# Two attention layers around a state-space block: the scan with tokens on partitions, its segment decays made beside the convolution, the decay rates spread by VectorE

## What is computed

```python
def _mamba2_block(x, norm_w, in_proj_w, conv_w, conv_b, dt_bias, A_log, D_skip, gnorm_w, out_proj_w):
    zxbcdt = _rms(x, norm_w) @ in_proj_w
    z = zxbcdt[..., :D_INNER]                       # 512 wide
    xBC = zxbcdt[..., D_INNER:D_INNER + CONV_DIM]   # 768 wide: x, B, C
    dt = jax.nn.softplus(zxbcdt[..., -H_M:] + dt_bias)        # 8 heads
    conv = conv_b + sum((padded[:, k:k + L, :] * conv_w[:, k] for k in range(D_CONV)))   # 4 taps
    xBC = jax.nn.silu(conv)
    decay = jnp.exp(dt * A)
    dbx = dt[..., None] * xh
    def step(h, inp):
        dec, u, bt, ct = inp
        h = h * dec[:, :, None, None] + u[..., None] * bt[:, None, None, :]
        return (h, jnp.einsum('bhpn,bn->bhp', h, ct))
    y = ys.transpose(1, 0, 2, 3) + D_skip[None, None, :, None] * xh
    u = _rms(y.reshape(b, L, D_INNER) * jax.nn.silu(z), gnorm_w)
    return resid + u @ out_proj_w
```

## Time and profile before

| | us |
|---|---|
| median of 3 runs | 9226.33 |
| lowest, highest | 9217.38, 9246.14 |
| the profiled execution, its own time | 9249.62 |
| the span of the profile | 9247.8 |
| busy: PE, DVE, ACT, POOL | 7938.6, 5014.7, 3326.8, 1960.8 |

### The profile page before, as it was taken

How to read it: one execution, slowest core, us unless ns; L and a number is a source line. 1 busy time by engine, 2 the same in 40 slices (tenths; PEclk the granted TensorE clock), 3 DMA queues, 4 the chain that set the end, 5 groups by cost and what they waited for, 6 DMA issues and landing times.

```text
span 9247.8 us, 129067 instructions
## 1 busy us (share of the span) xinstructions
PE 7938.6 (86%) x37700; PEld 3524.7 (38%) x38020; DVE 5014.7 (54%) x12781; ACT 3326.8 (36%) x4038; POOL 1960.8 (21%) x1802
## 2 busy tenths in 40 slices
PE   3979799897998979889798897979989798897988
PEld 0343433434333343333434334343343433334343
DVE  3555364654645556454564656536465464555546
ACT  0424334242342424424243342433424234242442
POOL 3040130302203031130311304013030221303113
PEclk5989889898998989989799898989989899898998
DMA  3142231323313132041422303223131330313213
GB/s 73 20 74 35 41 60 20 65 33 48 53 19 70 28 57 51 12 75 23 69 39 26 71 17 69 35 43 57 20 69 30 50 58 12 70 28 64 45 19 72
DMA packets 216597, 421.47 MB, mean 46 GB/s; under 512 B 35542, under 2 KB 126584, under 8 KB 215812
## 3 DMA queue, kind: packets, MB, share of 16 engines
q1 hardware_dynamic: 213841, 412.14, 25.9%
q10 hardware_dynamic: 2048, 0.53, 0.0%
HBM read 190.14 MB, written 8.51 MB: 21 GB/s over the span
## 4 chain that ended last, share of the span: by engine, by line
PE 59%; issue 14%; DVE 13%; DMA 6%; POOL 4%; ACT 2%; SPq 2%; DVEq 0%; ACTq 0%; POOLq 0%
PE ps L1004 13%; PE ps L941 10%; PE ps L975 8%; PE ps L977 6%; PE ps L903 5%; DVE mx L1588 5%; PE ps L979 4%; PE ps L1009 4%; DMA stage<-in_mask 3%; PE ps L1124 2%; DMA qst<-q1hl 2%; PE ps L960 2%; PE ps L1040 2%; DVE xc L1716 1%; ACT PR L1362 1%
## 5 line engine op out<-in xcount | busy, mean ns | idle before, releaser
L1362 ACT ACTIVATE PR<-ps 128x1024 f32<-128x1024 f32 x2496 | 2504.0, 1025 | 2634.8 <-PE ps L977 1514.2
L1559 DVE CUSTOM_DVE_ANT_0 ps<-ps,maskq 128x402 f32<-128x402 f32 x4203 | 2408.3, 587 | 1567.1 <-PE ps L941 1375.8
L1004 PE MATMUL ps<-PR,vbuf 128*32 128x512 f32 x9984 | 1356.6, 616 | 5.2 <-ACT PR L1362 5.2
L977 PE MATMUL ps<-maskk,identb 128*128 128x512 bf16 x3008 | 1147.6, 382 | 0.0
L941 PE MATMUL ps<-kst,qst 96*128 96x402 bf16 (+1 forms) x3115 | 1026.0, 342 | 115.6 <-DVE mx L1559 89.9
L1588 DVE TENSOR_REDUCE mx<-ps 128x2 f32<-128x804 f32 x1024 | 933.3, 988 | 314.1 <-PE ps L960 312.7
L960 PE MATMUL ps<-kst,qst 100*128 100x402 f32 x2048 | 753.3, 495 | 360.8 <-DMA qst<-q1hl 254.4
L975 PE MATMUL ps<-qst,kst 99*128 99x512 bf16 x2496 | 956.7, 383 | 7.3
L979 PE MATMUL ps<-qst,kst 102*128 102x512 f32 x1664 | 768.0, 526 | 100.3 <-ACT PR L1362 71.0
L941 PEld LDWEIGHTS ps<-kst,qst 96*128 96x128 bf16 x3115 | 282.4, 97 | 1209.7 <-DVE mx L1559 819.4
L722 POOL MEMSET qst<- 3x2048 f32 (+1 forms) x34 | 47.5, 1398 | 3117.7 <-PE ps L1004 3071.1
(11 more groups left out here) (194 smaller groups left out, 8046.4 us busy)
## 6 DMA issues: line engine op xcount, KB each, us to landing
kst<-khl SPq DMA_DIRECT2D x96, 800.5 KB, 17.0
kst<-khl SPq DMA_DIRECT2D x300, 200.1 KB, 7.6
stage<-in_maskt SPq DMA_DIRECT2D x204, 256.0 KB
stage<-in_mask SPq DMA_DIRECT2D x204, 201.0 KB
ctxs<-in_ctxt SPq DMA_DIRECT2D x17, 1601.0 KB, 9.7
qst<-q1hl SPq DMA_DIRECT2D x96, 256.0 KB, 12.1
win_s<-in_w_in SPq DMA_DIRECT2D x16, 1288.0 KB, 5.9
KS<-khl SPq DMA_DIRECT2D x102, 200.1 KB
```

What stands on the lines that cost most here:

```text
L977: mm = pe.matmul(o, identb[:, :], maskk[:, t, :], start=False, stop=True)
L1004: mm = pe.matmul(ps[32 * j:32 * j + 32, 6, :], l, PR[:, t % 2, j, :], start=(t == 0), stop=(t == KT - 1), tile_position=(0, 32 * j))
L1362: nc.scalar.activation(PR[:, t % 2, 2 * half:2 * half + 2, :], ps[:, 2 * half:2 * half + 2, :], ACT.Exp, scale=scale).then_inc(s_p, 1)
L1559: nc.vector.tensor_tensor_reduce(src, src, maskq[:, i, c0:c0 + w], 1.0, -3.0e38, ALU.add, ALU.max, mx[:, c, h * QT + i:h * QT + i + 1]).th ...
```

## The change

The scan's y now comes out with tokens on partitions, in the layout of the residual rows. The weight on the state is no longer a 128 x 1024 tensor per chunk but a factor per token and head (a third block of `dec`), applied after the matmul of C with `Hst`; the second sums, the second exponentials and the GpSimd product are gone. The skip term is a matmul with a diagonal matrix (`dskd`). z is projected with tokens on partitions. The gated rows are squared and summed on ScalarE, transposed by TensorE, copied by ScalarE and projected (`project_block(c)`) inside the loop.

All four triangles of decays are made beside the convolution: `aU` is filled by VectorE (`spread_a`, after the convolution steps in `A_STEPS`), and the exponentials go to `windows`, which lies on the memory of `qst`. The last tap and the bias of the convolution are made by ScalarE from PSUM, so VectorE runs three taps. All of `SECOND` is projected before the scan (`FILL0`, `FILL_AT`): 8 tiles before the transposes, then one after each projection j, three after the last.

Around it: the sums of the first attention are spread over partitions by four matmuls over 128 rows without waits between them, after the first tile of `project_out`; LayerNorm takes two operations a tile in place of three; the roots are taken in parts; the k parts on GpSimd come after the first roots; SyncE loads 2 mask pieces early and not 4, and waits for the sums (`s_D`), not for the end of the scan (`s_g`), before the next x; constant rows of the q stack, which `windows` overwrites, are written again from DRAM (`rows_q1`); the second q projection starts on three of the four row tiles.

```diff
--- before.py
+++ after.py
-        OUT_BANK = [0, 1, 3, 2]
+        OUT_BANK = [5, 7, 6, 3]
+        A_STEPS = [0, 3, 5, 6]
+        FILL0 = V_LN + 1
+        FILL_AT = [1] * (NCH + XT) + [3]
...
-        PIECE1, FRONT_PIECES, ROW1_STEP = 4, 2, 4
+        PIECE1, PIECE2, FRONT_PIECES, ROW1_STEP = 2, 4, 2, 4
...
-                sp.wait_ge(s_g, QT * (b + 1))
+                load_pieces(b, bn, 0, PIECE1, False)
+                sp.wait_ge(s_D, QT * (b + 1))
                 alone(sp)
                 load_xt(bn)
-                load_pieces(b, bn, 0, PIECE1, False)
                 sp.wait_ge(s_vfree, (b + 1) * KT)
                 alone(sp)
                 load_ctx(bn)
+                rows_q1(b)
                 for g in range(G1):
                     stack_q1(b, g)
...
-                if i == 0:
-                    pe.wait_ge(s_rs, b * NG + gi + 1)
-                else:
-                    pe.wait_ge(s_spread, n + i)
-                r = slice(32 * i, 32 * i + 32)
-                pe.matmul(ps[:, 7, i * P:(i + 1) * P], sel[r, :], rsm[r, :], start=True, stop=True,
-                          tile_position=(32 * i, 0)).then_inc(s_spread, 1)
+                pe.wait_ge(s_rs, b * NG + gi + 1)
+                for i in range(QT):
+                    mm = pe.matmul(ps[:, 7, i * P:(i + 1) * P], sel[:, i, :], rsm[:, :], start=True, stop=True)
+                mm.then_inc(s_spread, 1)
...
                     mm.then_inc(s_in, 1)
-                fill(V_IN)
+                    fill(FILL_AT[j])
+                    if NCH - 2 <= j < NCH + 2:
+                        window_sums(b, j - NCH + 2)
...
                 for c in range(QT):
                     cs = slice(c * P, (c + 1) * P)
                     nb = b * QT + c
                     if c > 0:
-                        window_sums(b, c)
+                        pe.wait_ge(s_h, LEAD + b * (QT - 1) + c)
...
+                        pe.matmul(ps[:, 3, :], xc[:, NCH - 1, cs], Hst[:, :], start=True, stop=True).then_inc(s_zi, 1)
...
                     for i in range(XT):
+                        pe.matmul(ps[:, 2, i * P:(i + 1) * P], xc[:, i, cs], dskd[:, i, :], start=(i == 0), stop=False)
                     pe.wait_ge(s_M, nb + 1)
                     pe.wait_ge(s_dx, nb + 1)
                     for h in range(HM):
+                        mm = pe.matmul(ps[:, 2, h * PD:(h + 1) * PD], window(c)[:, h, :], dx[:, h * PD:(h + 1) * PD],
+                                       start=False, stop=(h == HM - 1))
                     mm.then_inc(s_yp, 1)
                     if c < QT - 1:
+                        x_tokens(c + 1)
                         pe.wait_ge(s_dx2, b * (QT - 1) + c + 1)
...
+                        pe.matmul(ps[:, 4, :], btok[:, c, :], dx2[:, :], start=True, stop=True).then_inc(s_hp, 1)
+                    if c > 0:
+                        project_block(c - 1)
...
+                    nc.scalar.activation(xc[:, ch, :], ps[:, bank, :], ACT.Identity, bias=cb_c[:, ch:ch + 1],
+                                         scale=cw_c[:, ch * TAPS + TAPS - 1:(ch + 1) * TAPS])
                     nc.scalar.activation(rawc[:, n % 2, TAPS - 1:TAPS - 1 + T], ps[:, bank, :], ACT.Copy)\
                         .then_inc(s_rawcp, 1)
...
+                for n in range(NCH):
+                    gate(n)
+                    if n + 2 < NCH:
+                        copy_raw(n + 2)
+                    fill(FILL_AT[n + 3])
+                    if n == 0:
+                        act.wait_ge(s_dps, b + 1)
+                        nc.scalar.activation(dec[:, :, :].rearrange("p a n -> p (a n)"),
+                                             ps[:, 4, 0:3 * QT * HM], ACT.Exp).then_inc(s_dec, 1)
+                    elif n <= QT:
+                        window_decays(b, n - 1)
...
+                def spread_a(c):
+                    if c > 0:
+                        dve.wait_ge(s_D, b * QT + c)
+                    else:
+                        dve.wait_ge(s_a, b + 1)
+                    nc.vector.tensor_tensor(
+                        aU[:, :, :], aa[:, c, :].unsqueeze(2).broadcast_to([P, HM, P]),
+                        upto[:, :].unsqueeze(1).broadcast_to([P, HM, P]), ALU.mult).then_inc(s_au, 1)
+
                 for n in range(NCH + 1):
                     if n < NCH:
                         convolve(n)
+                    if n in A_STEPS:
+                        spread_a(A_STEPS.index(n))
                     if n >= 1:
                         gate_conv(n - 1)
```

More of the change, by code:

```diff
@@ L294, in xattn_mamba @@
         s_rstd = sem("s_rstd")
[L295 removed]
+        s_ln = [sem(f"s_ln{i}") for i in range(2)]
         s_sq = sem("s_sq")
@@ L1110, in _, with project_q1 @@
                 second = list(SECOND)
+                def project_q1(item, lo, hi):
+                    i = item[2]
+                    for k in range(DT):
+                        mm = pe.matmul(ps[:, pj_bank[item], lo:hi], wq1_s[:, k, i * P:(i + 1) * P], xn[:, k, lo:hi],
+                                       start=(k == 0), stop=(k == DT - 1))
+                    return mm
                 def fill(n):
@@ new lines, in _ @@
+                    if NCH - 2 <= j < NCH + 2:
+                        window_sums(b, j - NCH + 2)
+                assert not second
+                pe.wait_ge(s_xc, b * NCH + 2)
+                pe.wait_ge(s_vfree, (b + 1) * KT)
+                pe.wait_ge(s_rest, rests(b, K1[-1]) + 1)
+                for c in range(QT):
+                    cs = slice(c * P, (c + 1) * P)
+                    mm = pe.matmul(ps[:, 6, cs], xc[:, NCH - 2, cs], xc[:, NCH - 1, cs], start=True, stop=True)
+                mm.then_inc(s_G, 1)
```

536 lines of the change are left out of this document (275 added, 261 removed).

## The result

The changed kernel takes **8713.95 us** (median of 4 runs, 8706.96 to 8720.84) where the kernel before takes 9225.26 (4 runs beside it, 9217.38 to 9246.14): ratio **0.9442, 95% interval 0.9425 to 0.946**. That is 511 us or 31.9 us a batch less (33.9 between the two profiled executions, of which that of before lies above its median); 8835 was forecast, with a range of 8710 to 8970, so that the measured time lies 4 us inside its lower end. The profiled execution has a span of 8704.9 us (before: 9247.8).

The account below looks back on a forecast made before the run. Between the attentions no engine is full; chains from engine to engine bound the kernel. Terms sum to -24.5 us a batch, -392 over 16 batches: 8858 from the profiled 9249.6, or 8835 as median; range 8710 to 8970.

Parts of the forecast that it names:

- S3: Third stretch between the attentions, convolution and projections: 36.8 to 53.2 us, 16.4 dearer, held by ScalarE's k4 copy awaiting k transfers.
- S4: Fourth stretch, the scan's loop: 42.6 to 30.7 us, first interval 7.2 and then two of 8.4.
- S7: Seventh stretch, waiting for the q rows: 16.1 to 7.8 us, since they would meet an empty queue.
- S1: First stretch after the first attention, spreading the sums and projecting: 14.2 to 10.2 us, gain 4.0.
- S5: Fifth stretch, after the scan's loop: 16.7 to 9.6 us as sums of squares and three output projections leave.
- S10: Stretch of the next first attention up to the next reciprocal: no change forecast.
- the tail: End of the second attention: the same spreading edit as in S1, gain 2.6 us a batch.
- S2: Second stretch, normalization and roots: 24.3 to 17.3 us, from fewer VectorE operations, hidden roots and moved k parts.
- B: Rival: q rows no faster, the transfer itself takes the 16 us; 8968 us, chance 0.10.
- C: Rival: the k wait in S3 doesn't bind, the landing comes 9 us earlier; 8691 us, chance 0.12.
- D: Rival: slower than before, TensorE at 1.2 GHz after new waits; 9555 us, chance 0.05.
- E: Rival: S3 or S4 dearer on several sides, 5 us a batch more; 8915 us, chance 0.13.

Follow-up runs that it names:

- e1: Changed kernel with the sums spread as before: four small matmuls, each behind the one before, no projection tile in front; 8943.12 us, ratio 0.9679.
- e7: Changed kernel with the normalization of before: twelve VectorE operations behind the first root, one second root, k parts still behind the roots; 8815.52 us, ratio 0.9544.
- e5: Changed kernel with SyncE's queue order of before: four mask pieces early, next x only after the scan's last gated product; 8762.33 us, ratio 0.9481.
- e11: Changed kernel with all four output projections behind the scan's loop, gated products keeping four places; 8843 us, ratio 0.9567.
- e6: Kernel before the change with only the new spreading of the sums, at all five places; 8983.53 us, ratio 0.9725.
- e3: Changed kernel with k4 to k7 projected after the last three v tiles; 8697.28 us, ratio 0.9419.
- e4: Changed kernel with k4 to k7 projected two tiles later, only the last v tile behind them; 8698.25 us, ratio 0.9419.
- e8: Changed kernel with k4 to k7 two tiles later and the third and fourth segment-decay sums one step later; 8636.15 us, ratio 0.9347.
- e10: The e8 kernel with the four spreads of the decay rates on GpSimd instead of VectorE; 8560.17 us, ratio 0.9271.
- e9: Changed kernel with only the third and fourth segment-decay sums one step later, k4 to k7 left in place; 8708.34 us, ratio 0.9427.

## Why the prediction was right, and where it wasn't

**The sum.** The undone parts cost 229 (e1), 102 (e7), 48 (e5) and 129 us (e11), together 508 of the 511 us. They needn't add up, and e1 and e6 differ by 28 us for one edit; but the size suggests that what is left, the scan with its decays moved beside the convolution (S3 dearer by 19.2, S4 cheaper by 14.9 of which e11's overlap is a part), is near zero by itself. That is argued and not shown: no run has the new scan alone, or the old scan with the rest. The forecast gave the edits around the scan 2.6 + 4.0 + 7.0 + 8.3 = 21.9 of its 24.5 us a batch, so it had most of the gain in the right part of the kernel, but not in the right shares: the spread is worth 14.3 us a batch for 6.6, the norm without the k parts 6.4 for 4.05, the queue 3.0 for 8.3. Part of it is luck: S3 and S7 came out 2.8 and 1.8 us dearer and S1, S4, S5 and S8 to S10 cheaper, and the time landed at the edge of the range.

**S1 and the tail** are the terms that were mis-sized: 5.8 and 4.3 for 4.0 and 2.6. By their own rows they come to 3.8 (1.17 + 2.90 + 0.9, less 1.2 for the new spread) and 2.2 (1.07 + 2.33 - 1.2), so the miss is larger than it looks. In the kernel before the clock had fallen behind the chain of small matmuls (0.76 over S1), and the forecast took the projection behind them from the earlier trace rows as work at the rate shown. S10's 4.5 us were left out altogether, and so were S8's 2.0; e1 and e6 show S10's (5.2 and 4.7).

**S2** came to 6.2 of 7.0 (its four terms as stated add up to 6.6). e7 confirms the operations and roots (4.4 for 4.05); some 1.8 are left for the k parts, which had been given 2.5, but their effect alone wasn't tried.

**S3** has the right length (55.8 for 53.2) by a wrong composition. The wait was found at its place and size, 10.65 us for 9. The chain behind it runs as told. What failed is the price: "Without it S3 would be 44", but e3 and e4 take it away and S3 falls by 4, not 9, to 52.1 and 51.4. "What decides is a wait that the profile of before doesn't show" is thus half true: of TensorE's two long waits one hangs on it, and the other on the place of VectorE's spread. TensorE's list had been added up at full clock to 41 us; it takes 47.5, and 43 in e8, where hardly a wait is left to pull the clock down.

**S4 and S5**: rounds of 5.9, 7.9 and 7.9 for 7.2, 8.4 and 8.4, so S4 is 2.9 us shorter than forecast; the loop was taken apart rightly, with each piece rounded up. S5 is 7.8 for 9.6.

**S6 and S7**: +0.4 for 0, and -6.5 for -8.3. The q rows' wait fell from 16.48 to 9.7 us, "about 8" had been said, and the cause given for it was two fifths of it (e5). The prediction put the late context down to pieces that GpSimd converts late; the first piece was late because it landed behind the k transfers.

**The rivals.** B (the q rows aren't faster) is out. C (the k wait doesn't bind, 8691) is nearest to the measured time and to what e3 shows, though the reason it gave, an earlier landing, is false: the wait is there and is in part covered. D (half clock throughout) is out, S4 ran at 1.00; but its mechanism in small is in the misses of S1, S3, S8 and S10: the sum behind the wait of 3.50 us takes 3.78 us in place of 1.9. The Trainium skill (TensorE: Matmul & The Clock Gate, Part 1) says that the clock drops when the engine idles and returns under sustained work; the trace agrees, with 0.50 of full clock from 1014 to 1018, behind that wait, and 1.00 again from 1020 to 1026. E is out: the loop came cheaper, not dearer.

**The contention.** One microsecond of S3 was given to k parts beside taps. A tap with nothing beside it takes 0.75 us, and the mean of 18 is 814 ns with the parts (e8): 1.2 us, as said. GpSimd's large products cost more, 997 ns (e10).

## What to carry to other kernels

Cost a small chain of dependent instructions at every place where it runs, above all inside the loops of the engine that has no slack, and add the work behind it at the lower clock if TensorE waited for it: here the least conspicuous edit was worth half of the gain. A wait found in the trace has its full price only if nothing else holds the same work up; take two overlapping waits away together, since either alone (e4, e9) shows nothing and both (e8) 78 us. Before moving an operation to the faster engine, look at what stands ahead of it in that engine's order: a GpSimd product of 2.2 us that starts at once served TensorE better than a VectorE one of 1.2 us behind its taps.
